# Second norm's factors stored with each row of attention's output; expert lists by one matmul a tile

## Chip, cores and metric

The kernel runs on one core of one Trainium2 chip. The time is that of one execution on the device, in microseconds (us). TensorE is PE, VectorE DVE, ScalarE ACT, GpSimd POOL, and SyncE, which here only issues DMAs, SP.

## The reference, cut to what matters

Rows of 256 floats (D) are embedded, go through attention with a residual, and then through a mixture of 8 experts, in which every expert takes the same number of rows (T / E):

```
h = tok(x)
h = h + attn(layernorm(h))                      # h1: 32 sequences x 512 tokens = 16384 rows
f = layernorm(h)                                # first norm of the expert layer: (x - m) / sqrt(v + eps)
norm = layer_norm(f, g, b)                      # second norm, of the rows already normed
scores = norm @ centroids.T
for e in range(8):                              # C = 2048 rows each, without those taken before
    s = where(taken, -inf, scores[:, e]); idx = top_k(s, C); taken[idx] = True
routed = f[idx]
out = routed + gelu(layer_norm(routed) @ w1 + b1) @ w2 + b2
h = h + out (put back at the rows' places)
```

Both norms are of the same row, so both come from one mean m and one variance v of the h1 row: y = (h1 - m) * ((1 + eps) v + eps^2)^-0.5 is what the expert's matmuls get (gain and bias g, b are put in later), and h1 * (1 + r) - m * r, with r = (v + eps)^-0.5, is what is added to the expert's result. These are the row's factors: two powers, and the two products with -m.

## The kernel before

All engines run in one program, each with its own instruction list, and hand over by semaphores (`wait_ge`). Work is in tiles of 128 rows (one row a partition); there are NT = 128 tiles, TS = 4 for each of the 32 sequences.

**Attention.** A loop over sequences; each step is a plan of ten halves (slots 0 to 9) written out by hand. The plan names tasks; PE makes them, ACT ("A") or DVE ("D") takes the result out of one of three PSUM banks. What the change touches is the task WO, the output product of a tile: tile 0 in slot 8, tiles 1, 2 and 3 in slots 0, 2 and 4 of the next step. In `dve_misc` (L1202 to L1218) DVE takes WO: it makes the tile's unscaled scores (L1206), h1 = residual + product (L1210), statistics (L1213), mean and variance (L1215), and stores (1 + eps) v + eps^2 in column n of `ve_all` (L1217). Before that DVE waits until the h1 buffer of two tiles ago is stored. SP (`store`) first issues, per half, the small transposed DMAs of MX tasks (`low`, L466 and L469), then the store of the h1 tile to `h1_rows` in HBM (L476), when DVE has made it. POOL's share of a step is, in this order, the gather of the next rows (L515, slots 5 to 8) and the norm of the step after next (`pool_norm`, L522, L528, L530, slots 6 to 9; its xn is what PE transposes at L784 in slot 0 of the next step).

**Between.** When all tiles are stored, POOL takes one power over all of `ve_all` (L621), DVE multiplies the scores by it (L1493), adds the constant (L1495), and then makes the list of the first expert alone (`dve_choice`): eight digits of 4 bits, for each a count of the rows over 15 candidates (L1251, 15 operations, summed over partitions by one PE matmul, L836), then cut, ties, positions, and the list. For the list DVE writes one-hot tensors of [128, 128 tiles, 16] bf16, ohP (place in the tile) and ohT (tile number) from ohA (L1292, L1295, L1296), and in 8 parts the tensor ohB of 16 tiles (L1302, two buffers). For each tile PE multiplies ohB's 128 columns as weights with ohP and with ohT (L857): 32 matmuls of 16 columns for each part, summed in one PSUM tile, which DVE converts to row numbers (`idx_next`, L1307).

**Experts.** Each of 8 experts has GR = 4 groups of GT = 4 tiles. For a group PE does 8 slots m of the first layer (L911; ACT's Gelu L728), then for each tile q the second layer (L924, slots 8 + q). While it does, the next group is prepared: POOL gathers its tiles (L539) into one half of `hrow`; DVE takes statistics of all four (`dve_stats`, L1322 to L1329) when they are there; POOL takes eight powers (`pool_power`, L583); DVE makes biases (`dve_scales`, L1333, L1334); ACT writes y and the residual part of each tile (`act_rows`, L700, L702); PE transposes y (`pe_rows`, L898), behind q = 0, 1 and 2, but for an expert's last group behind q = 2 and q = 3; ACT takes it out as hT (L717). DVE adds the residual to the result (`orow`, L1368), POOL adds b2 (L567) and scatters it (L571), and frees the buffer (L579), for which DVE waits.

The choice of the next expert's rows is spread over the slots by two tables, `pe_at` and `dve_at`. In groups 0 and 1: digits and counts, with the statistics in slot 5 and the scales in slot 7; slot 0 of each begins with a digit and a count right behind the last group's `orow`. In group 2: the rest of the choice, and the first list parts at slots 9 to 11. In group 3, slot 0, DVE does the last four parts and the numbers at once; PE has its parts in slots 0 to 3 and 5; statistics and scales come behind the first and second `orow`, and the gather of the next expert's first group waits for the numbers. So the order on each engine is fixed by hand.

## Time and profile before

| | us |
|---|---|
| median of 3 runs | 3180.93 (3177.55 to 3189.85) |
| the profiled execution | 3194.65 |
| its span | 3192.8 |
| PE busy | 2786.0 |
| DVE busy | 1804.9 |
| ACT busy | 1275.4 |
| POOL busy | 873.6 |

The span is what the profile's stretches and shares refer to; 1.85 us of the execution lie around it. PE is busy for 87% of the span, but matmuls are pipelined, so that does not say that it is at its peak. A row of a timeline gives start, length, engine and line, what is written and read, and in brackets the idle time of the engine before it with what ended it.

### The profile page before, as it was taken

The page shows a single profiled execution, that of the slowest core. Times are in us where ns is not written, and L with a number is a line of the kernel's source. Part 1 is how long each engine was busy: PE and PEld are TensorE (multiplying, and loading weights), DVE is VectorE, ACT ScalarE, POOL GpSimd, SP SyncE. Part 2 cuts the span into 40 slices and gives each one's busy share as a digit, 9 for nine tenths or more (in the row PEclk, how much of TensorE's full clock was granted, in tenths as well). Part 3 has the DMA queues.
Part 4 walks back from the last instruction along what each step waited for, and adds up shares of the span by engine and source line. Part 5 has one row for each costly group of instructions (what it writes and reads, how often), then busy time and mean ns, then how long its engine had stood idle before and what let it go on. Part 6 is the DMA issues. An engine that isn't in the chain of part 4 may idle for free. (4 is left out here: it accounts for less than half of the span.)

```text
span 3192.8 us, 118687 instructions
## 1 busy us (share of the span) xinstructions
PE 2786.0 (87%) x49160; PEld 1942.8 (61%) x49160; DVE 1804.9 (57%) x5978; ACT 1275.4 (40%) x2665; POOL 873.6 (27%) x938
## 2 busy tenths in 40 slices
PE   3899989989989989989989998059899999999998
PEld 1566666666666666666666666036565665655666
DVE  3555555555555555555556554667567676665720
ACT  1454444444444444444444442023333333343433
POOL 2212122122122112112112110224353443434443
PEclk9999999999999999999999998569999999999999
DMA  2000000000000000000000000000111101111020
GB/s 62 20 24 22 21 23 24 20 22 21 23 22 20 21 21 24 21 21 24 19 23 24 21 19 15 30 17 31 62 46 49 55 31 63 41 47 61 28 66 27
DMA packets 56398, 98.21 MB, mean 31 GB/s; under 512 B 10332, under 2 KB 41000, under 8 KB 55752
## 3 DMA queue, kind: packets, MB, share of 16 engines
q0 software_dynamic: 18624, 50.88, 5.6%
q1 hardware_dynamic: 37256, 40.07, 3.8%
q8 instruction: 368, 6.03, 0.8%
q14 instruction: 150, 1.23, 0.1%
HBM read 55.78 MB, written 33.55 MB: 28 GB/s over the span
## 5 line engine op out<-in xcount | busy, mean ns | idle before, releaser
L515 POOL DMA_INDIRECT rows<-in_tok_table,idx_now x132 | 138.0, 1045 | 1442.3 <-DVE hres L1154 1368.5
L911 PE MATMUL banks<-hT,w 128*128 128x512 f32 x1024 | 485.0, 622 | 16.1 <-ACT hT L717 12.1
L1176 DVE TENSOR_REDUCE mx<-banks 128x8 f32<-128x1024 f32 x256 | 301.5, 1219 | 204.3 <-PE banks L1014 200.9
L691 ACT ACTIVATE probT<-banks 128x1024 f32<-128x1024 f32 x256 | 262.6, 1026 | 229.8 <-PE banks L1058 229.8
L728 ACT ACTIVATE hid<-banks,b 128x512 f32<-128x512 f32 x256 | 175.2, 687 | 439.1 <-PE banks L911 439.0
L911 PEld LDWEIGHTS banks<-hT,w 128*128 128x128 f32 x1024 | 192.9, 197 | 229.6 <-issue 217.1
L1071 PEld LDWEIGHTS V_ps<-Ve,probT 128*64 128x64 f32 x4096 | 268.9, 147 | 24.9 <-issue 24.9
L1071 PE MATMUL V_ps<-Ve,probT 128*64 128x17 f32 x4096 | 281.8, 217 | 1.4 <-issue 1.4
L1071 PE MATMUL V_ps<-Vo,probT 128*64 128x17 f32 x4096 | 282.0, 217 | 0.2 <-issue 0.2
L1071 PEld LDWEIGHTS V_ps<-Vo,probT 128*64 128x64 f32 x4096 | 268.9, 147 | 0.3 <-issue 0.3
L1251 DVE TENSOR_SCALAR_CACHE_REDUCE hits<-act_s,cval 128x128 bf16<-128x128 f32 x960 | 261.6, 342 | 12.9 <-issue 10.7
L924 PE MATMUL M_ps<-w,hid 128*128 128x256 f32 x1024 | 233.3, 382 | 0.0
L924 PE MATMUL V_ps<-w,hid 128*128 128x256 f32 x1024 | 231.5, 380 | 0.0
L924 PEld LDWEIGHTS V_ps<-w,hid 128*128 128x128 f32 x1024 | 193.1, 190 | 38.4 <-issue 15.3
L924 PEld LDWEIGHTS M_ps<-w,hid 128*128 128x128 f32 x1024 | 191.8, 192 | 23.7
L1197 DVE TENSOR_TENSOR r<-M_ps,sg 128x256 f32<-128x256 f32 x128 | 54.4, 425 | 248.5 <-PE M_ps L799 247.6
L567 POOL TENSOR_TENSOR orow<-orow,b 128x256 f32<-128x256 f32 x128 | 127.1, 993 | 238.1 <-DVE orow L1368 236.7
L1052 PE MATMUL banks<-Qt,Kt 32*64 32x128 f32 x4096 | 184.7, 282 | 0.0
L657 ACT ACTIVATE low<-M_ps 8x256 f32<-8x256 f32 x128 | 47.7, 372 | 326.3 <-PE M_ps L793 326.3
L1052 PEld LDWEIGHTS banks<-Qt,Kt 32*64 32x64 f32 x4096 | 164.1, 132 | 22.7 <-issue 3.8
L571 POOL DMA_INDIRECT out_rows<-orow,idx_cur x128 | 144.4, 1128 | 110.5 <-POOL orow L567 77.3
L1054 PE MATMUL banks<-Qt,Kt 32*64 32x64 f32 x4096 | 173.4, 227 | 0.1
(228 smaller groups left out, 5885.3 us busy)
## 6 DMA issues: line engine op xcount, KB each, us to landing
h_rows<-h SPq DMA_DIRECT2D x128, 128.0 KB, 2.0
w<-in_w SPq DMA_DIRECT2D x16, 1024.0 KB, 5.9
Qt<-low SPq DMA_DIRECT2D x256, 4.0 KB
rows<-in_tok_table,idx_now POOLq DMA_INDIRECT x132, 3.5
out_rows<-orow,idx_cur POOLq DMA_INDIRECT x128, 2.5
cst<-in_tables SPq DMA_DIRECT2D x1, 1060.5 KB
Gq<-lowl SPq DMA_DIRECT2D x64, 8.0 KB
b<-in_b SPq DMA_DIRECT2D x8, 128.0 KB, 5.0
```

The source lines that it names most:

```text
L515: nc.gpsimd.indirect_dma_start(rows[:, t, :], None, ins["tok_table"], bass.IndirectOffsetOnAxis(idx_now[:, t:t + 1], 0)).then_inc(s_rows[t ...
L567: nc.gpsimd.tensor_tensor(out=orow[:, q % 2, :], in0=orow[:, q % 2, :], in1=b2[:, :], op=ALU.add).then_inc(s_add, 1)
L571: nc.gpsimd.indirect_dma_start(out, bass.IndirectOffsetOnAxis(idx_cur[:, g * GT + q:g * GT + q + 1], 0), orow[:, q % 2, :], None).then_inc ...
L691: nc.scalar.activation(dst[:, 2 * pair:2 * pair + 2, :], banks[:, 2 * pair:2 * pair + 2, :], ACT.Exp).then_inc(s_exp, 1)
L728: nc.scalar.activation(hid[:, m, :], S_ps[m % 2][:, 0:GT * P], ACT.Gelu_apprx_tanh, bias=b1[:, m:m + 1]).then_inc(s_hid, 1)
L911: mm = nc.tensor.matmul(S_ps[m % 2][:, 0:GT * P], w1[:, c, m * P:(m + 1) * P], hT[g % 2][:, c, :], start=c == 0, stop=c == KC - 1)
L924: mm = nc.tensor.matmul(O_ps[q % 2][:, 0:D], hid[:, m, q * P:(q + 1) * P], w2[:, m, :], start=m == 0, stop=m == FC - 1)
L1052: nc.tensor.matmul(banks[side[0], g, n * P:(n + 1) * P], k[:, W + at_:P + at_], q[:, at_:at_ + P], start=False, stop=n == G - 1)
L1054: nc.tensor.matmul(banks[side[1], g, n * P:n * P + W], k[:, at_:W + at_], q[:, at_:at_ + W], start=False, stop=False)
L1071: nc.tensor.matmul(V_ps[side[a], h * OW:(h + 1) * OW], probT[t % 2][:, g, n * P + a * W:n * P + (a + 1) * W], vals[:, t, h, :], start=True ...
L1176: nc.vector.tensor_reduce(tops.rearrange("p (g h) -> p g h", g=2), banks[:, 2 * pair:2 * pair + 2, :].rearrange("p g (h k) -> p g h k", h= ...
L1251: ins_ = nc.vector.tensor_scalar(hits[:, c, :], act_s[:, :], cval[:, c:c + 1].bitcast(F32), None, ALU.is_ge, ALU.add, accum_out=counts[:, ...
```

## The change

Each h1 row gets four more columns (1,040 bytes in place of 1,024): the two powers (the second with 1 added) and the two products with -m. DVE now writes both variances of the tile (`ve1`), and POOL, at the end of the slot of each WO, takes the two powers, the two products, the product of the tile's eight scores with the first power, and adds 1 (`pool_factors`). SP's store waits for this (`s_fac`). The factors come back with the gathered row, so `act_rows` waits for the gather itself and reads its scales and biases in the row; `dve_stats`, `dve_scales`, `pool_power` and the power over all tiles are gone, and the score product on DVE too: DVE waits for `s_score` of the last tile. ohP and ohT become the two halves of one tensor, ohN [128, 128 tiles, 2, 16], so that a list part is 16 matmuls of 32 columns, and the numbers are a copy of one half of PSUM and an addition of the other.

```diff
+RW = D + 4
...
-        h1_rows = nc.dram_tensor("h1_rows", [TOK, D], F32, kind="Internal").ap()
+        h1_rows = nc.dram_tensor("h1_rows", [TOK, RW], F32, kind="Internal").ap()
...
-        h1 = sb("h1", [P, 2, D])
+        h1 = sb("h1", [P, 2, RW])
...
-        mv1 = sb("mv1", [P, 2])
-        ve_all = sb("ve_all", [P, NT])
-        rs_all = sb("rs_all", [P, NT])
+        mv1 = sb("mv1", [P, 2, 2])
+        ve1 = sb("ve1", [P, 2, 2])
+        eps = sb("eps", [P, 2, 2])
...
-        ohP = sb("ohP", [P, NT, CT], BF16)
-        ohT = sb("ohT", [P, NT, CT], BF16)
+        ohN = sb("ohN", [P, NT, 2, CT], BF16)
...
-        hrow = sb("hrow", [P, 2, GT, D])
+        hrow = sb("hrow", [P, 2, GT, RW])
...
-        s_gr = [sem(f"s_gr{q}") for q in range(GT)]
-        s_var2 = sem("s_var2")
-        s_rs2 = sem("s_rs2")
-        s_scales = sem("s_scales")
+        s_gr = [[sem(f"s_gr{j}{q}") for q in range(GT)] for j in range(2)]
...
-                            sp.wait_ge(s_mD, m.out(task))
+                            sp.wait_ge(s_fac, TS * (b - lag(task)) + t + 1)
                             sp.dma_start(h1_tiles[:, bass.ds(TS * (b - lag(task)) + t, 1), :],
                                          h1[:, t % 2, :].unsqueeze(1)).then_inc(s_h1out[t % 2], 16)
...
+        def pool_factors(pool, n, t):
+
+            own = h1[:, t % 2, :]
+            pool.wait_ge(s_var1, n + t + 1)
+            nc.gpsimd.tensor_tensor(out=own[:, D:D + 2], in0=ve1[:, t % 2, :], in1=mhalf[:, :].to_broadcast([P, 2]),
+                                    op=ALU.pow).then_inc(s_rs1, 1)
+            pool.wait_ge(s_rs1, n + t + 1)
+            stand(pool)
+            nc.gpsimd.tensor_scalar(own[:, D + 2:D + 4], own[:, D:D + 2], mv1[:, t % 2, 0:1], -1.0,
+                                    ALU.mult, ALU.mult).then_inc(s_nm1, 1)
+            new = score[:, :, bass.ds(n + t, 1)]
+            nc.gpsimd.tensor_tensor(out=new, in0=new, in1=own[:, D:D + 1].unsqueeze(1).to_broadcast([P, E, 1]),
+                                    op=ALU.mult).then_inc(s_score, 1)
+            pool.wait_ge(s_nm1, n + t + 1)
+            stand(pool)
+            nc.gpsimd.tensor_scalar(own[:, D + 1:D + 2], own[:, D + 1:D + 2], 1.0, None, ALU.add).then_inc(s_fac, 1)
...
-                bass.IndirectOffsetOnAxis(idx[:, col:col + 1], 0)).then_inc(s_gr[q], 16)
+                bass.IndirectOffsetOnAxis(idx[:, col:col + 1], 0)).then_inc(s_gr[half][q], 16)
...
-                if g + 1 < GR:
-                    pool_power(pool, gi + 1)
...
-                    if (g, q) == (GR - 1, 1) and not last:
-                        pool_power(pool, gi + 1)
...
+                    for task in half:
+                        name, t = task
+                        if name == "WO" and m.here(task):
+                            pool_factors(pool, TS * (b - lag(task)), t)
...
-            pool.wait_ge(s_var1, NT)
-            nc.gpsimd.tensor_tensor(out=rs_all[:, :], in0=ve_all[:, :], in1=mhalf[:, :].to_broadcast([P, NT]),
-                                    op=ALU.pow).then_inc(s_rs1, 1)
...
-            pool_power(pool, 0)
...
-            if q == 0:
-                act.wait_ge(s_scales, gi + 1)
...
+            row = hrow[:, half, q, :]
+            act.wait_ge(s_gr[half][q], 16 * pair + 16)
             if q >= 2:
                 act.wait_ge(s_yT, GT * gi + q - 1)
-            nc.scalar.activation(y2[:, q % 2, :], hrow[:, half, q, :], ACT.Identity, scale=rs2[:, 0, q:q + 1],
-                                 bias=nmr[:, 0, q:q + 1]).then_inc(s_y2, 1)
-            nc.scalar.activation(hrow[:, half, q, :], hrow[:, half, q, :], ACT.Identity, scale=r1[:, q:q + 1],
-                                 bias=nmr[:, 1, q:q + 1]).then_inc(s_scaled, 1)
...
+            nc.scalar.activation(y2[:, q % 2, :], row[:, 0:D], ACT.Identity, scale=row[:, D:D + 1],
+                                 bias=row[:, D + 2:D + 3]).then_inc(s_y2, 1)
+            nc.scalar.activation(row[:, 0:D], row[:, 0:D], ACT.Identity, scale=row[:, D + 1:D + 2],
+                                 bias=row[:, D + 3:D + 4]).then_inc(s_scaled, 1)
...
-        LPS = M_ps[1][:, 0:CT]
+        LPS = M_ps[1][:, 0:2 * CT]
...
                 for j in range(LT):
-                    for half in (ohP, ohT):
-                        first_, last_ = k == 0 and j == 0 and half is ohP, k == LC - 1 and j == LT - 1 and half is ohT
-                        mm = nc.tensor.matmul(LPS, ohB[:, k % 2, j, :], half[:, k * LT + j, :],
-                                              start=first_, stop=last_)
+                    mm = nc.tensor.matmul(LPS, ohB[:, k % 2, j, :],
+                                          ohN[:, k * LT + j, :, :].rearrange("p a r -> p (a r)"),
+                                          start=k == 0 and j == 0, stop=k == LC - 1 and j == LT - 1)
                 mm.then_inc(s_used, 1)
...
-                  (2, 5): [("stats", 0)], (2, 6): [("list", 0)], (2, 7): [("scales", 0)], (2, Q0): [("places", 0)],
+                  (2, 6): [("list", 0)], (2, Q0): [("places", 0)],
                   (2, Q0 + 1): [("list", 1)], (2, Q0 + 2): [("list", 2)], (2, Q0 + 3): [("list", 3)],
-                  (3, 0): [("list", 4), ("list", 5), ("list", 6), ("list", 7), ("numbers", 0)],
-                  (3, Q0 + 1): [("stats", 0)], (3, Q0 + 2): [("scales", 0)]}
+                  (3, 0): [("list", 4), ("list", 5), ("list", 6), ("list", 7), ("numbers", 0)]}
...
-            dve_at[g, 5] = [("stats", 0)]
...
-            dve_at[g, 7] = [("scales", 0)]
...
-                chain(dve, nc.vector.bn_aggr(mv1[:, :], st1[:, :]), base)
-
-                nc.vector.tensor_scalar(ve_all[:, bass.ds(TS * bt + t, 1)], mv1[:, 1:2], 1.0 + EPS, EPS * EPS,
-                                        ALU.mult, ALU.add).then_inc(s_var1, 1)
+                chain(dve, nc.vector.bn_aggr(mv1[:, t % 2, :], st1[:, :]), base)
+
+                nc.vector.scalar_tensor_tensor(out=ve1[:, t % 2, :], in0=eps[:, 0, :], scalar=mv1[:, t % 2, 1:2],
+                                               in1=eps[:, 1, :], op0=ALU.mult, op1=ALU.add).then_inc(s_var1, 1)
...
-                nc.vector.tensor_scalar(ohP[:, :, :], ohA[:, :, :], c_part, None, ALU.mult)
-                nc.vector.scalar_tensor_tensor(out=ohT[:, :, :], in0=ohA[:, :, :], scalar=float(P),
+                nc.vector.tensor_scalar(ohN[:, :, 0, :], ohA[:, :, :], c_part, None, ALU.mult)
+                nc.vector.scalar_tensor_tensor(out=ohN[:, :, 1, :], in0=ohA[:, :, :], scalar=float(P),
                                                in1=laneb[:, 0:NT].unsqueeze(2).to_broadcast([P, NT, CT]),
                                                op0=ALU.mult, op1=ALU.mult).then_inc(s_ohA, 1)
...
-                nc.vector.tensor_copy(idx_next[:, :], LPS).then_inc(s_next, 1)
+                chain(dve, nc.vector.tensor_copy(rank[:, 0:CT], LPS[:, 0:CT]), base)
+                nc.vector.tensor_tensor(idx_next[:, :], rank[:, 0:CT], LPS[:, CT:2 * CT], ALU.add).then_inc(s_next, 1)
...
-        def dve_stats(dve, gi, half, base):
-            if not (isinstance(gi, int) and gi == 0):
-                dve.wait_ge(s_scaled, GT * gi)
-            for q in range(GT):
-                dve.wait_ge(s_gr[q], 16 * gi + 16)
-                nc.vector.bn_stats(st2[:, q, :], hrow[:, half, q, :])
-            chain(dve, nc.vector.memset(r1[:, :], 1.0), base)
-            stand(dve)
-            for q in range(GT):
-                ins_ = nc.vector.bn_aggr(mv2[:, q, :], st2[:, q, :])
-            chain(dve, ins_, base)
-            nc.vector.tensor_scalar(ve2[:, 0, :].unsqueeze(2), mv2[:, :, 1:2], 1.0 + EPS, EPS * EPS, ALU.mult, ALU.add)
-            nc.vector.tensor_scalar(ve2[:, 1, :].unsqueeze(2), mv2[:, :, 1:2], EPS, None, ALU.add).then_inc(s_var2, 1)
-
-        def dve_scales(dve, gi, base):
-            dve.wait_ge(s_rs2, gi + 1)
-            nc.vector.tensor_scalar(r1[:, :], rs2[:, 1, :], 1.0, None, ALU.add)
-            nc.vector.scalar_tensor_tensor(out=nmr[:, :, :], in0=mv2[:, :, 0].unsqueeze(1).to_broadcast([P, 2, GT]),
-                                           scalar=-1.0, in1=rs2[:, :, :], op0=ALU.mult, op1=ALU.mult)\
-                .then_inc(s_scales, 1)
...
+            for j in range(2):
+                nc.vector.memset(eps[:, 0, j:j + 1], (1.0 + EPS, 1.0)[j])
+                chain(dve, nc.vector.memset(eps[:, 1, j:j + 1], (EPS * EPS, EPS)[j]))
...
-            dve.wait_ge(s_rs1, 1)
-            chain(dve, nc.vector.tensor_tensor(score[:, :, :], score[:, :, :],
-                                               rs_all[:, :].unsqueeze(1).to_broadcast([P, E, NT]), ALU.mult), base)
+            dve.wait_ge(s_score, NT)
             chain(dve, nc.vector.tensor_tensor(score[:, :, :], score[:, :, :],
                                                kb[:, :].unsqueeze(2).to_broadcast([P, E, NT]), ALU.add), base)
...
-            dve_stats(dve, 0, 0, base)
-            dve_scales(dve, 0, base)
```

## Rows read from the trace of the kernel before

**Rows 1.** Stretches: busy us (instructions) of each engine, granted clock, DMA share, GB/s.

```profile
1000.00:1900.00 900.00, 825.48 (x20460) 596.34 (x20460) 500.48 (x1253) 405.51 (x886) 180.06 (x240) 0.95 0.08 22
2400.00:2800.00 400.00, 375.43 (x2045) 247.65 (x2044) 266.37 (x1198) 150.81 (x288) 175.90 (x155) 0.98 0.14 45
```

The engines of these columns are PE, its weight loads, DVE, ACT and POOL.

**Rows 2.** Timeline of DVE and POOL at attention's end (start us, length us).

```profile
2000.61 0.15 DVE L1217 TENSOR_SCALAR ve_all<-mv 128x1 f32<-128x1 f32 x1
2001.89 20.75 POOL L621 TENSOR_TENSOR rs_all<-ve_all,mhalf 128x128 f32<-128x128 f32 x1 [134.47 <-DMA h_rows<-h]
2022.78 1.22 DVE L1493 TENSOR_TENSOR score<-score,rs_all 128x1024 f32<-128x1024 f32 x1 [22.02 <-POOL rs_all L621]
```

**Rows 3.** Timeline before the first expert's first matmul.

```profile
2110.51 0.43 DVE L1322 BATCH_NORM_STATS2 st<-hrow 128x6 f32<-128x256 f32 x1 [0.83 <-DMA hrow<-h_rows,idx_next]
...
2118.16 0.60 ACT L700 ACTIVATE y<-hrow,nmr,rs 128x256 f32<-128x256 f32 x1
...
2120.86 1.22 PE L911 MATMUL banks<-hT,w 128*128 128x512 f32 x1 [1.36 <-ACT hT L717]
```

**Rows 4.** PE's waits in the expert stage, 2121 to 3192 (total us, times, longest).

```profile
PE M_ps L836 <- DVE hits L1251: 31.9, 17, 3.1
PE banks L898 <- ACT y L700: 12.2, 20, 2.2
```

**Rows 5.** Single lines over the whole run: count, duration ns min/median/max.

```profile
L522 POOL TENSOR_TENSOR rs<-ve,mhalf x128: 549/582/586, 53.9 to 1865.2; 128x1 f32<-128x1 f32 x128
L583 POOL TENSOR_TENSOR rs<-ve,mhalf x32: 1660/1672/3639, 2111.8 to 3139.5; 128x8 f32<-128x8 f32 x32
L1295 DVE TENSOR_SCALAR ohP<-ohA,cst x8: 753/753/754, 2081.1 to 3022.1; 128x2048 bf16<-128x2048 bf16 x8
L1302 DVE TENSOR_TENSOR ohB<-laneb,rlow x64: 2277/2283/2820, 2084.0 to 3044.3; 128x2048 bf16<-128x2048 bf16 x64
L1261 DVE TENSOR_TENSOR thr<-thr,delta x64: 158/160/1102, 2031.4 to 3004.0; 128x1 int32<-128x1 int32 x64
L1210 DVE TENSOR_TENSOR h<-hres,M_ps x128: 410/414/417, 135.0 to 1999.4; 128x256 f32<-128x256 f32 x128
```

**Rows 6.** Timeline of one attention step around the slots 8 and 9.

```profile
1020.26 0.15 DVE L1217 TENSOR_SCALAR ve_all<-mv 128x1 f32 x1
...
1022.41 0.19 POOL L528 TENSOR_TENSOR std<-ve,rs 128x1 f32<-128x1 f32 x1 [0.25 <-POOL rs L522]
1022.57 1.22 POOL L530 TENSOR_SCALAR xn<-hres,mv,rs 128x256 f32<-128x256 f32 x1
...
1032.89 0.48 PE L784 MATMUL M_ps<-cst,xn 128*128 128x128 f32 x1
```

**Rows 7.** Timeline of PE in the second expert: starts of short bf16 matmuls.

```profile
2329.78 0.23 PE L840 MATMUL M_ps<-equal,beforeb 128*128 128x128 bf16 x1
2329.84 0.22 PE L841 MATMUL M_ps<-equal,onesb 128*128 128x128 bf16 x1
...
2348.72 0.17 PE L857 MATMUL M_ps<-ohP,ohB 128*128 128x16 bf16 x1
...
2349.50 0.17 PE L857 MATMUL M_ps<-ohT,ohB 128*128 128x16 bf16 x1
```

**Rows 8.** Timeline of ACT and PE behind the Gelus of two groups.

```profile
2340.68 0.69 ACT L728 ACTIVATE hid<-banks,b 128x512 f32<-128x512 f32 x1 [1.03 <-PE banks L911]
2343.36 0.60 ACT L700 ACTIVATE y<-hrow,nmr,rs 128x256 f32<-128x256 f32 x1 [1.99 <-DVE nmr L1334]
2344.99 0.33 PE L898 MATMUL banks<-cst,y 128*128 128x128 f32 x1 [0.54 <-ACT y L700]
...
2387.15 0.60 ACT L700 ACTIVATE y<-hrow,nmr,rs 128x256 f32<-128x256 f32 x1 [9.30 <-DVE nmr L1334]
```

**Rows 9.** SP's waits in attention, 1000 to 1900 (total us, times, longest).

```profile
SPq L469 <- ACT low L657: 511.0, 60, 9.4
```

**Rows 10.** DMA issues: KB each, median us from issue to landing.

```profile
hrow<-h_rows,idx_next POOLq DMA_INDIRECT x64, 2.8
```

More of the change, by code:

```diff
@@ L190, in tower @@
         b1_all = sb("b1_all", [P, E, FC])
-        st2 = sb("st2", [P, GT, 6])
-        mv2 = sb("mv2", [P, GT, 2])
-        ve2 = sb("ve2", [P, 2, GT])
-        rs2 = sb("rs2", [P, 2, GT])
-        r1 = sb("r1", [P, GT])
-        nmr = sb("nmr", [P, 2, GT])
         wq = sba("wq", [P, KC, D])
@@ L319, in tower @@
         s_rs1 = sem("s_rs1")
+        s_nm1 = sem("s_nm1")
+        s_fac = sem("s_fac")
+        s_score = sem("s_score")
         s_std = sem("s_std")
@@ L692, in act_exp, with act_rows, act_group @@
                                  ACT.Exp).then_inc(s_exp, 1)
-        def act_rows(act, gi, q, half):
-            if q == 0:
-                act.wait_ge(s_scales, gi + 1)
+        def act_rows(act, gi, pair, q, half):
+            row = hrow[:, half, q, :]
+            act.wait_ge(s_gr[half][q], 16 * pair + 16)
             if q >= 2:
                 act.wait_ge(s_yT, GT * gi + q - 1)
-            nc.scalar.activation(y2[:, q % 2, :], hrow[:, half, q, :], ACT.Identity, scale=rs2[:, 0, q:q + 1],
-                                 bias=nmr[:, 0, q:q + 1]).then_inc(s_y2, 1)
-            nc.scalar.activation(hrow[:, half, q, :], hrow[:, half, q, :], ACT.Identity, scale=r1[:, q:q + 1],
-                                 bias=nmr[:, 1, q:q + 1]).then_inc(s_scaled, 1)
-        def act_group(act, gi, g):
-            act_rows(act, gi, 0, g % 2)
+            nc.scalar.activation(y2[:, q % 2, :], row[:, 0:D], ACT.Identity, scale=row[:, D:D + 1],
+                                 bias=row[:, D + 2:D + 3]).then_inc(s_y2, 1)
+            nc.scalar.activation(row[:, 0:D], row[:, 0:D], ACT.Identity, scale=row[:, D + 1:D + 2],
+                                 bias=row[:, D + 3:D + 4]).then_inc(s_scaled, 1)
+        def act_group(act, gi, pair, g):
+            act_rows(act, gi, pair, 0, g % 2)
             for q in range(GT):
                 if q + 1 < GT:
-                    act_rows(act, gi, q + 1, g % 2)
+                    act_rows(act, gi, pair, q + 1, g % 2)
                 act_transposed(act, gi, q, g)
@@ L730, in act_expert @@
                 if g + 1 < GR or not last:
-                    act_group(act, gi + 1, g + 1 if g + 1 < GR else 0)
+                    act_group(act, gi + 1, GR // 2 * e + (g + 1) // 2, g + 1 if g + 1 < GR else 0)
         @block.scalar
@@ L765, in _ @@
             nc.scalar.activation(scr[:, :], c_ident[:, 0:1], ACT.Copy).then_inc(s_hid, 2)
-            act_group(act, 0, 0)
+            act_group(act, 0, 0, 0)
             with act.Fori(0, E - 1) as e:
@@ L1343, in dve_expert @@
                 gi = GR * e + g
-                more = g + 1 < GR or not last
                 def parts(slot):
                     for part, k in dve_at.get((g, slot), []):
-                        if part == "stats":
-                            if more:
-                                dve_stats(dve, gi + 1, (g + 1) % 2, base)
-                        elif part == "scales":
-                            if more:
-                                dve_scales(dve, gi + 1, base)
-                        elif part == "numbers now":
+                        if part == "numbers now":
                             dve.wait_ge(s_free, 2 + CT * e)
@@ L1367, in dve_expert @@
                     dve.wait_ge(s_free, GT * gi + q + 1)
-                    nc.vector.tensor_tensor(orow[:, q % 2, :], O_ps[q % 2][:, 0:D], hrow[:, g % 2, q, :],
+                    nc.vector.tensor_tensor(orow[:, q % 2, :], O_ps[q % 2][:, 0:D], hrow[:, g % 2, q, 0:D],
                                             ALU.add).then_inc(s_fin, 1)
@@ L1500, in _ @@
                 dve_choice(dve, 0, part, k, base)
[L1501 to L1502 removed]
             base += CH["n"]
             CH["n"] = 0
[L1505 removed]
+            PER2 = 6 * DIGITS + 24
             with dve.Fori(0, E - 1) as e:
```

11 lines of the change are left out of this document (3 added, 8 removed).

## The prediction, made before the changed kernel ran

> **What bounds the kernel now.** I read the stages first, then the start of the expert stage as a chain, then what TensorE (PE) waits for in the experts. In attention (nearly 2,000 of the 3,192.8 us) PE is busy 825 of 900 us and POOL only 180; in the experts (from about 2,121 us) PE is busy 375 of 400 us. Between attention's last variance at 2000.61 and PE's first expert matmul at 2120.86 lie 120 us [rows 2, 3], in which PE has only the short matmuls of the choice. That stretch is one chain: POOL takes a power over all 128 tiles at once, 20.75 us, and DVE stood idle 22.02 us until it came; then DVE multiplies the scores, 1.22 us [rows 2], and chooses the first expert's rows with nothing beside it. Then four tiles are gathered; the last is there at 2110.51, but ACT writes its y only at 2118.16, because statistics, power and scales stand between; PE starts at 2120.86 [rows 3]. From there PE waits 31.9 us for the counts (DVE hits) and 12.2 us for y [rows 4]. So time is to be had where PE is short of work at the start, or where PE has less to do in the experts. DVE's work is worth nothing by itself.
>
> **The change, part by part.**
>
> 1. *The power over all tiles goes.* Last tile's variance is ready at 2000.61 + 0.15 = 2000.76 and the second score operation starts behind 2022.78 + 1.22 = 2024.00 [rows 2]. Now POOL does for this tile a power of 2 elements, a two-element product, then the 8-element score product, and DVE goes on at s_score. Power: 582 ns for 1 element and 1,672 for 8 [rows 5], 0.16 a further element, so 0.74. The wait behind it 0.25 and a small operation 0.19 [rows 6]. The score product has no row: between 0.19 (1 element) and 1.67 (8 elements of power); I take 0.3, since 256 elements take only 1.22 [rows 6]. Two hand-overs at 0.14 each (22.78 less 2001.89 + 20.75). Sum 1.8: DVE goes on at about 2002.5, gain **21.5** (20.1 to 21.6).
>
> 2. *Statistics of group 0 go.* ACT needs only the tile. y of the fourth tile starts at 2110.5 in place of 2118.16, and what follows it is the same; the other three are ready before. Gain **7.6** [rows 3]. The numbers cost one small DVE operation more (0.2), the last list part of PE is 0.4 shorter: **+0.2**. The first half of the one-hot tensor, 0.753 us now [rows 5], is written in runs of 16 elements; between 0.75 and the 2.28 of its neighbours of the same size without speed-up [rows 5]. I take 0.75, the runs being still contiguous; the end costs 1.5 once (in the other seven experts DVE is ahead there).
>
> 3. *Lists with one moving operand.* 8 experts x 8 parts x 32 matmuls become 16 of 32 columns. A part's 31 starts take 2349.50 - 2348.72 = 0.78 us, 25 ns each at 16 columns; with 128 columns two starts lie 60 ns apart [rows 7]. Straight between them 32 columns is 30 ns. If each column cost its share, 16 columns could not take 25 ns beside 60 for 128: a floor shows, so I take 25, part 0.80 to 0.40. The Trainium skill, "TensorE: Matmul & The Clock Gate", section "Wait — 56ns, not 53.3ns?", gives about 25 ns also for 32 columns; no row here shows it. The first expert's parts lie behind DVE's ohB (2.28 us each [rows 5]) and give nothing. The other 56 are in PE's own stream: 56 x 0.40 = **22.4** (17 at 30 ns, 0 if the price goes with columns). With list parts of 0.4 a slot on PE is 2.15 us (now 2.6), shorter than an ohB, so four parts in a row could catch up with DVE; but DVE has 3 us or more less ahead of them (statistics, the wait for scales), and enters group 3 earlier. I put nothing there; the end is 0.5 us in each of 7 experts, 3.5.
>
> 4. *Statistics, power and scales of the 31 other groups go.* DVE is lighter by some 3 us a group (four statistics of 0.43 [rows 3] and eight small operations), worth nothing as such: the long waits for hits come right behind a group's last orow (digit and count in slot 0), before the statistics, and stay. But ACT stands 1.99 us before y in one group and 9.30 us in the next for nmr [rows 8]; now it starts as its last Gelu ends (2341.37) or the gather lands. y of tile 1 is then ready three operations of 0.6 later, 2343.2, and PE asks for it at 2344.45 (2344.99 less its wait of 0.54 [rows 8]). So the y waits go: **12** of 12.2 [rows 4]. Next late are hT (the last two tiles' transposes directly before the next expert; unchanged) and hits. POOL also no longer holds a scatter behind var2.
>
> 5. *Attention, DVE.* One fused operation of 2 elements in place of one of 1, 154 ns [rows 6]: at most 0.08 x 128 off PE's path; DVE is busy 500 of 900 us [rows 1]. The setup gets four memsets, two waited for: **-0.4**, an estimate from small operations of 0.15 to 0.2; ends 0 and -1.
>
> 6. *Attention, POOL.* Four operations a tile, 0.74 + 0.25 + 0.19 + 0.3 + 0.25 + 0.19, about 1.9 us; 128 x 1.9 = 245 us on an engine that is 80% idle [rows 1]. Order matters: factors of tile 0 (slot 8) now stand before the norm of tile 3 (slot 9). Their variance is there at 1020.41; POOL is free of the second-last norm at 1021.6, so xn of tile 3 ends at 1023.8 + 1.9 = 1025.7, and PE reads it at 1032.89 [rows 6]: 7 us to spare. At the other slots POOL is idle. DVE itself waits for none of it before the end.
>
> 7. *SP and DMA.* The h1 store now waits for POOL, 2 us later. Behind it on SP is the next low store; SP waits 8.5 us on average for each of those (511.0 / 60 [rows 9]), which covers it. The buffer is wanted two tiles later, at 2,000 / 128 = 15.6 us a tile. Rows are 1,040 B in place of 1,024: gathers take 2.8 us to land [rows 10], issue paces them, and only group 0's last is exposed. The Trainium skill, "DMA: Bandwidth & Descriptors", section "How a descriptor splits into AXI transactions", speaks against such rows: rows that do not start at a 256-byte boundary fetch bytes they do not use, here up to a quarter more (an estimate from 1,040 B at such offsets). By that rule the last gather would land up to 0.7 us later and the sum be that much smaller; no row shows it.
>
> **Sum.** 21.5 + 7.6 + 0.2 + 22.4 + 12 - 0.4 = 63.3. The profiled execution took 3194.65 us and would take 3131.4. It lies 13.7 above the median of the runs, 3180.93; the gains are counts of work and not shares, so I take them off the median: **3118**.
>
> **Rivals.**
> - *Lists give nothing* (32 columns cost twice 16): for it, that no row has 32 columns; against it, the floor seen at 25 ns. 3194.65 - 40.9, or on the median 3140. Chance 0.08.
> - *DVE becomes what PE waits for in the experts*: the time cut from lists and y is waited for at the next count or ohB, so that only the start's 29.3 - 0.4 stays: 3152. For it, hits is already the largest wait [rows 4]; against it, its waits start at a group's end and no cut lies between that and the count. Chance 0.10.
> - *Slower: VectorE and POOL hold each other up in attention.* A DVE operation of 160 ns took 1,102 beside a POOL instruction, and a POOL power of 1.67 took 3.64 beside DVE [rows 5]. If each tile's factors held DVE up by 0.94 us where PE waits for h or the maxima, 128 x 0.94 = 120: 3118 + 120 = 3238. It decides from (63 + 16) / 128 = 0.62 us a tile, where the kernel would be slower by 0.5%. Against it: beside POOL's norms h took 410 to 417 ns, always [rows 5]. Chance 0.04. The Trainium skill's "GPSIMD Engine Reference", section "Specifications", says that the two share SBUF interfaces when DVE has two SBUF inputs or a 2-port mode, which is this mechanism; the trace agrees for the experts' 2,048-element operations and not for attention's.
> - *More than the sum*: with the lighter DVE and POOL a third of the hits waits goes too (10 of 31.9): 3108. Chance 0.10.
>
> **How the numbers follow.** The forecast has 0.68: its own range is 3110 to 3126 (lists at 30 ns, one-hot at 2.28, ohB 3.5: up; runs of before reach 3.4 below their median: down). The range 3103 to 3142 takes in the cases of more and of lists without gain. About 0.5%, 16 us, is what a measurement can tell from no change. All cases but the slower one gain over 16 us, less 0.03 for something unseen in attention that eats the gain: faster 0.93, same 0.03, slower 0.04.
>
> **What would show it.** Right: no POOL operation of 20 us before the scores, DVE's score operation 2 us behind the last variance; PE's first expert matmul 29 us nearer to attention's end; L857's successor 1,024 times, 25 ns apart; PE waits for y near nothing; hits near 30 us; attention's windows with the same PE busy and length. Wrong: matmul starts 50 ns apart, hits or ohB waits risen by 20 to 30 us, or a longer attention stage, with PE waiting for h or xn.

## The result, and the profile after

| | before | after |
|---|---|---|
| median of 4 runs each, us | 3185.39 (3177.55 to 3196.62) | 3092.39 (3087.99 to 3101.93) |
| profiled execution, us | 3194.65 | 3101.93 |
| expert stage (first first-layer matmul to the end), us | 1071.9 | 1007.4 |
| PE busy, us | 2786.0 | 2745.5 |
| DVE busy, us | 1804.9 | 1738.9 |
| POOL busy, us | 873.6 | 976.6 |

The ratio is 0.9709 (95%: 0.9668 to 0.9751): faster by 2.9%, 93 us. I had forecast 63 us and a range that ended at 3103; the measured 3092 lies 11 us below it. The direction was right and the size was not; about 30 us came from something that I had not counted. Those 30 lie in the expert stage: it gained 64.5 us where items 3 and 4 had 34.4. Attention's last variance starts at 2000.02, and before at 2000.61 [rows 2].

The two stretches of [rows 1], after the change:

```profile
1000.00:1900.00 900.00, 827.55 (x20700) 597.13 (x20699) 507.73 (x1264) 412.10 (x899) 270.02 (x484) 0.96 0.08 22
2400.00:2800.00 400.00, 385.33 (x1752) 252.29 (x1751) 257.52 (x1128) 161.87 (x306) 163.62 (x155) 0.99 0.16 51
```

In attention's 900 us POOL is busy for 90 us more; PE's busy time moves by 2 us and DVE's by 7, and attention does not end later. In the experts PE is busy 385 of 400 us (375 before).

Timeline of DVE and POOL at attention's end, which answers to [rows 2]:

```profile
2000.02 0.22 DVE L1215 SCALAR_TENSOR_TENSOR ve<-eps,mv 128x2 f32<-128x2 f32 x1
2000.33 0.72 POOL L531 TENSOR_TENSOR h<-ve,mhalf 128x2 f32<-128x2 f32 x1 [4.64 <-DVE ve L1215]
2001.26 0.27 POOL L535 TENSOR_SCALAR h<-h,mv 128x2 f32<-128x2 f32 x1 [0.20 <-POOL h L531]
2001.48 0.21 POOL L538 TENSOR_TENSOR score<-score,h 128x8 f32<-128x8 f32 x1
2001.83 1.22 DVE L1467 TENSOR_TENSOR score<-score,kb 128x1024 f32<-128x1024 f32 x1 [1.58 <-POOL score L538]
```

The power of 20.75 us is gone; DVE goes on 1.81 us behind the last variance's start, 1.59 behind its end, where I had 1.8.

Timeline before the first expert's first matmul, which answers to [rows 3]:

```profile
2085.97 0.60 ACT L702 ACTIVATE y<-hrow 128x256 f32<-128x256 f32 x1
...
2088.33 0.60 ACT L702 ACTIVATE y<-hrow 128x256 f32<-128x256 f32 x1 [0.58 <-DMA hrow<-h_rows,idx_next]
2088.84 0.58 ACT L704 ACTIVATE hrow<-hrow 128x256 f32<-128x256 f32 x1
...
2089.33 0.78 ACT L719 ACTIVATE hT<-banks,ln 128x128 f32<-128x128 f32 x2
2090.02 0.59 ACT L702 ACTIVATE y<-hrow 128x256 f32<-128x256 f32 x1
...
2092.71 1.21 PE L909 MATMUL banks<-hT,w 128*128 128x512 f32 x1 [1.36 <-ACT hT L719]
```

Here the fourth y does not start when its tile lands, as I had it: the third tile's y comes late, and its residual part and an hT stand on ACT between the two. From the numbers' first operation to PE's first matmul it takes 12.01 us in place of 18.09, a gain of 6.1 and not 7.6.

What PE waits for in the expert stage (2093 to the end), which answers to [rows 4]:

```profile
PE M_ps L838 <- DVE hits L1249: 20.5, 16, 1.9
PE banks L909 <- ACT hT L719: 12.1, 8, 1.6
PE banks L909 <- ACT hid L730: 1.1, 2, 0.8
```

y has left the table, as forecast. But hits (PE waiting for a count), which I said would stay at 31.9, stands at 20.5, and hid (PE waiting for a Gelu's result) fell from 4.0 to 1.1. That is the lead.

### The profile page after: what moved, and what is told of

Same layout as the page of the kernel before. It is cut to its first block and busy times, and to the rows that moved or that the text cites. A ratio compares the mean times of both kernels' runs of the same rounds, so it can differ in the third digit from the quotient of the medians.

```text
span 3100.1 us, 116908 instructions
## 1 busy us (share of the span) xinstructions
PE 2745.5 (89%) x48136; PEld 1915.2 (62%) x48136; DVE 1738.9 (56%) x5573; ACT 1277.5 (41%) x2665; POOL 976.6 (32%) x1417
## 5 line engine op out<-in xcount | busy, mean ns | idle before, releaser
L909 PE MATMUL banks<-hT,w 128*128 128x512 f32 x1024 | 477.6, 613 | 13.4 <-ACT hT L719 12.1
L531 POOL TENSOR_TENSOR h<-ve,mhalf 128x2 f32<-128x2 f32 x128 | 95.2, 744 | 916.8 <-DVE ve L1215 916.8
L922 PEld LDWEIGHTS M_ps<-w,hid 128*128 128x128 f32 x1024 | 190.3, 190 | 23.6
```

What stands on the lines that cost most here:

```text
L531: nc.gpsimd.tensor_tensor(out=own[:, D:D + 2], in0=ve1[:, t % 2, :], in1=mhalf[:, :].to_broadcast([P, 2]), op=ALU.pow).then_inc(s_rs1, 1)
L909: mm = nc.tensor.matmul(S_ps[m % 2][:, 0:GT * P], w1[:, c, m * P:(m + 1) * P], hT[g % 2][:, c, :], start=c == 0, stop=c == KC - 1)
L922: mm = nc.tensor.matmul(O_ps[q % 2][:, 0:D], hid[:, m, q * P:(q + 1) * P], w2[:, m, :], start=m == 0, stop=m == FC - 1)
```

## Where the missing 30 us are: one turn of the loop, side by side

PE's timeline at the third expert's start, the kernel before:

```profile
2394.67 3.70 PE L911 MATMUL banks<-hT,w 128*128 128x512 f32 x8 [1.56 <-ACT hT L717]
2398.87 1.99 PE L911 MATMUL banks<-hT,w 128*128 128x512 f32 x4 [0.51 <-ACT hid L728]
2403.93 0.20 PE L836 MATMUL M_ps<-counts,onesb 128*128 128x15 bf16 x1 [3.07 <-DVE hits L1251]
2404.01 8.31 PE L911 MATMUL banks<-hT,w 128*128 128x512 f32 x12
2412.16 0.17 PE L836 MATMUL M_ps<-counts,onesb 128*128 128x15 bf16 x1
```

and after the change:

```profile
2346.06 5.69 PE L909 MATMUL banks<-hT,w 128*128 128x512 f32 x12 [1.56 <-ACT hT L719]
2352.82 0.18 PE L838 MATMUL M_ps<-counts,onesb 128*128 128x15 bf16 x1 [1.07 <-DVE hits L1249]
2352.90 5.41 PE L909 MATMUL banks<-hT,w 128*128 128x512 f32 x12
2358.41 0.18 PE L838 MATMUL M_ps<-counts,onesb 128*128 128x15 bf16 x1
```

Two things differ. The wait for the first count is 3.07 and now 1.07. And the twelve matmuls behind it take 8.31 us before and 5.41 after: a loss that stands in no table of waits. The stretches of the kernel before show what it is (the last three columns are PE's granted clock, DMA share and GB/s):

```profile
2394.67:2404.00 9.33, 5.75 (x13) 2.19 (x13) 5.29 (x37) 3.23 (x4) 3.28 (x4) 0.95 0.44 145
2404.00:2406.00 2.00, 2.00 (x4) 0.97 (x5) 1.63 (x12) 0.00 (x0) 1.56 (x2) 0.50 0.45 131
2406.00:2408.00 2.00, 2.00 (x4) 0.89 (x3) 2.00 (x17) 0.17 (x1) 0.00 (x0) 0.50 0.23 66
```

Behind the long wait PE runs at a granted clock of 0.50 (1.2 GHz) for over 5 us. After the change the same place has 1.00. "Low clock" below is the sum of (1 - granted clock) over stretches of 1 us of the expert stage: 23.6 us before and 13.8 after. In the kernel before the clock fell at or just behind all six waits of about 3 us (in three of them before the wait had ended); after the change it fell behind none of those of 1.07; and it fell behind the waits of about 2 us in group 1 sometimes (three of seven before, five of seven after). That is no fixed rule: in a_shift25, below, it did not fall at one wait of 2.80 us. One fall costs PE about 1.4 us: group 1's first layer took 16.52 us before without one and 17.89 after with one, with the same wait in both.

Why is the count earlier? DVE's timeline at the same turn, before:

```profile
2396.55 0.17 DVE L1341 COPY b<-b_all 128x8 f32 x1 [3.42 <-issue]
...
2400.85 0.35 DVE L1251 TENSOR_SCALAR_CACHE_REDUCE hits<-act_s,cval 128x128 bf16<-128x128 f32 x1 [1.92 <-issue]
```

and after:

```profile
2347.45 0.17 DVE L1319 COPY b<-b_all 128x8 f32 x1 [2.92 <-issue]
```

At each turn DVE stands 3 to 4 us in front of the loop's first operation and waits for nothing that the profile shows. Before the change it stands a second time, 1.9 us, between the fourth and the fifth of 15 count operations, whose instructions did not change at all. In sum, for DVE over the expert stage of the kernel before:

```profile
DVE b L1341 <- issue: 21.5, 6, 4.1
...
DVE hits L1251 <- issue: 10.7, 6, 1.9
```

The second line is gone after the change; the first is 18.7. **Theory "place of the code":** DVE fetches its program in pieces; at a jump back the piece with the loop's start is fetched, and the next comes later. Before the change a piece ended some 22 instructions behind the loop's start, within the first count. The change took, by my count of the two programs, 25 instructions out ahead of the loop, so the piece reaches that much further, to a place where DVE waits for PE anyway. **Rival "lighter loop":** the gap went because statistics, scales and powers left the experts.

## Experiments

Labels with a_ start from the changed kernel, with b_ from the one before. Ratios are to the kernel before on the same chip. Attention's code is the same in all a_ kernels, yet its last mean and variance came anywhere from 1982.8 to 2012.2 us in their profiled executions; so medians carry several us of it, and I read sizes from the expert stage. That stage, the waits and the low clock are each read from one profiled execution, so a difference of a few us, of the size of two or three falls of the clock, is not to be leaned on.

| kernel | median us | ratio (95%) | expert stage, us | hits wait, us | low clock, us |
|---|---|---|---|---|---|
| before | 3185.4 | | 1071.9 | 31.9 | 23.6 |
| after | 3092.4 | 0.9709 (0.9668 to 0.9751) | 1007.4 | 20.5 | 13.8 |
| a_shift25 | 3123.9 | 0.9793 (0.9747 to 0.9839) | 1022.8 | 31.4 | 19.3 |
| a_shift64 | 3106.4 | 0.9736 (0.9704 to 0.9768) | 1007.8 | 21.1 | 13.8 |
| a_shift40 | 3127.3, one run | | 1032.4 | 42.4 | 19.6 |
| b_shift30 | 3169.6 | 0.9954 (0.9926 to 0.9982) | 1061.2 | 24.4 | 13.4 |
| b_lists | 3162.4 | 0.9918 (0.9887 to 0.9950) | 1055.0 | 30.8 | 16.9 |
| a_oldlists | 3122.5 | 0.9784 (0.9758 to 0.9810) | 1030.4 | 21.9 | 11.7 |
| a_slots | 3076.3 | 0.9648 (0.9623 to 0.9674) | 982.8 | 4.4 | 6.7 |
| a_turn | 3098.8 | 0.9721 (0.9687 to 0.9756) | 1007.1 | 14.1 | 22.3 |
| a_best | 3072.5 | 0.9614 (0.9584 to 0.9644) | 970.3 | 6.1 | 5.6 |
| b_slots | 3151.4 | 0.9902 (0.9885 to 0.9919) | 1042.5 | 10.7 | 5.8 |

### Moving the loop's code and nothing else

```diff
+        pad = sb("pad", [P, 25])
...
+            for j in range(25):
+                nc.vector.memset(pad[:, j:j + 1], 0.0)
             dve.wait_ge(s_score, NT)
```

**a_shift25.** 

> The changed kernel with 25 tiny memsets (128x1) of an unused tile on DVE, directly before DVE's wait for the last tile's scores, so that the code of the expert loop starts 25 instructions later in DVE's program, at the place (1,451st) that it has in the kernel before; nothing in the loop differs. The memsets themselves: 25 x 0.06 = 1.5 us, where DVE stands idle for 1.58. Theory 'place of the code': the gap of 1.8 us in the first count of each expert (DVE waiting for 'issue', 10.7 us in 6 times in the kernel before, none in the changed one) depends on where the loop's code lies. It comes back at the fifth of the 15 count operations, PE's wait for hits in group 0 goes from 1.07 to about 3, PE's granted clock falls to 0.50 behind it (1.7 us lost), so 6 x (1.8 + 0.3 + 1.7) = 23: 3115 us. Rival 'lighter loop': the gap went because statistics, scales and powers left the experts; then the memsets change nothing, 3092 to 3094, no issue gap in the count.

**a_shift64** (64 in place of 25). 

> The same with 64 memsets in place of 25. Direct cost 64 x 0.06 = 3.8 us less the 1.58 that DVE is idle: 2.3 us. Theory 'place of the code': if the gap comes where one piece of the code ends and the next has not arrived, the piece now ends before the loop's first instruction, no gap in the count, 3092 + 2.3 = 3095. Rival 'any longer program' (each added instruction ahead of the loop costs): gap at least as with 25 memsets, 3115 or more. Rival 'lighter loop': 3095 as well, so that only the pair with 25 memsets tells it from the first theory.

**b_shift30** (30, ahead of `dve.wait_ge(s_rs1, 1)` in the kernel before). 

> The kernel before with 30 memsets of an unused tile on DVE, directly before DVE's wait for the power over all tiles, where DVE stands idle for 22 us: they cost nothing. Theory 'place of the code': the piece of code that ends 22 instructions behind the loop's first one in the kernel before now ends before it; the gaps in the count (10.7 us in 6) go, hits waits fall by about 11 to about 21, the clock stays at 1.00 behind the first count of an expert, and the time is 3185 - 23 = 3162 (ratio 0.993). Rival 'lighter loop': 3185, gap and waits as before.

DVE's timeline at the third expert's start with 25 memsets:

```profile
2355.82 0.17 DVE L1320 COPY b<-b_all 128x8 f32 x1 [2.94 <-issue]
...
2359.94 0.09 DVE L1250 DVE_READ_ACCUMULATOR hits<-act_s,cval 128x1 bf16 x1 [1.49 <-issue]
```

With 25 tiny memsets, executed once, 90 us ahead of the experts, the gap is back, now in front of the read behind the fifth count operation; the loop's code is the same. Hits waits rise to 31.4 and the expert stage by 15.4 us. With 64 the gap is absent and the stage is 1007.8 against 1007.4. In the kernel before, 30 take the gap away and bring 10.7 us. "Lighter loop" foresaw no effect in the first and third and is out. The medians go the same way: b_shift30's ratio, 0.9954, has 1 outside its interval. That of a_shift64, 3106.4, is 11 us over the 3095 that I expected; its attention was 12 us longer than the changed kernel's in the profiled executions.

My sizes were too large (23 foreseen, 15.4 and 10.7 measured). I took 1.7 us for a fall of the clock, which costs 1.4. With 25 memsets the low clock also rose by only 5.5 us, where six falls of 1.7 would be 10.2: at two of the six first counts the clock stayed up, and it fell behind four of group 1's waits where it had fallen behind five. In b_shift30 the waits in group 0 fell by 11.2 us, as foreseen (17.6 to 6.4), and the low clock by 10.2; but the waits in group 1 rose from 1.9 to about 2.35 us each, 3 us in sum, and those for y, hid, ohB and equal by 3.5 together.

**a_shift40** (40 memsets). 

> The changed kernel with 40 memsets. With 25 the issue gap stood after the fifth count operation, 23 instructions behind the loop's first one when each count operation is counted as two (the operation and the read of its sum). Theory 'place of the code': with 15 more it stands 8 instructions behind the first one, before cand (L1246), again six times and 1.6 us long; the count is as late as with 25, so the expert stage is 1022 to 1026 us (1022.8 with 25, 1007.8 with 64). Rival 'the gap belongs to the count operations' (their own pipeline, the load of the DMA queues at that time): it stays between count operations, or does not appear.

DVE's timeline there, third expert:

```profile
2350.32 0.17 DVE L1320 COPY b<-b_all 128x8 f32 x1 [2.94 <-issue]
...
2354.33 0.17 DVE L1246 TENSOR_TENSOR cand<-digits,thr 128x15 int32<-128x15 int32 x1 [3.45 <-issue]
```

The place is right to the instruction, but the gap is not 1.6 us: it is 3.4 to 3.7, and the stage 10 us longer than with 25 memsets. The rows tell why. From b's copy to the end of the gap it is 4.01 us here, 4.12 with 25 memsets and 4.30 in the kernel before (4.0 to 4.3 at nearly all turns). So the next piece comes about 4 us behind the loop's start, wherever the piece ends; the nearer its end, the longer DVE stands. The DMA view of the kernel before for 2397 to 2401 has this line, a transfer of instructions (8 KB) within the gap:

```profile
q14 instruction: 1, 0.01, 0.5%
```

The traces' single packets show more. At each of the six turns, in all twelve kernels, a packet of this queue starts 1.6 to 2.5 us behind the first operation. In all 30 turns with a gap (before, a_shift25, a_shift40, b_lists, b_slots) DVE goes on 1.85 to 1.93 us after that packet's start, and a second packet starts within 5.0 us; in the kernels without a gap there is no second one so soon. The DMA view for the 5 us behind b's copy, in the kernel before (2396.5 to 2401.5) and after (2347.4 to 2352.4):

```profile
q14 instruction: 2, 0.02, 1.0%
q14 instruction: 1, 0.01, 0.5%
```

That DVE waits for this transfer is thus more than a guess from the gap's place, though the queue's lines do not name the engine that it serves.

The Trainium skill, "Runtime: NRT & Kernel Launch", section "Instruction fetch mechanics", says that instructions come by DMA in blocks, and that a taken branch to a target outside the window forces a fetch. The wait at each turn and the gap's place agree with it. It also says that crossing a block's end is mostly hidden; behind a jump it was not here, 0.9 to 3.7 us each time.

### The two halves of the change

```diff
-                    for half in (ohP, ohT):
...
-                        mm = nc.tensor.matmul(LPS, ohB[:, k % 2, j, :], half[:, k * LT + j, :],
-                                              start=first_, stop=last_)
+                    mm = nc.tensor.matmul(LPS, ohB[:, k % 2, j, :],
+                                          ohN[:, k * LT + j, :, :].rearrange("p a r -> p (a r)"),
+                                          start=k == 0 and j == 0, stop=k == LC - 1 and j == LT - 1)
```

**b_lists** (the lists alone, in the kernel before). 

> The kernel before with the lists alone changed (one tensor ohN, 16 matmuls of 32 columns a part, the numbers by a copy and an addition). Theory 'parts of 0.40': in PE's own stream 7 x 8 parts take 0.40 in place of 0.81 us, 56 x 0.41 = 23: 3185 - 23 = 3162; hits waits 31.9, issue gaps in the count 10.7 and y waits about 12 stay. Rival 'lists did more': the shorter lists alone also shortened the hits waits or the y waits, 3185 - 23 - 10 or more = 3152 or less. Rival 'DVE holds the list': PE catches up with DVE's ohB in group 3 and waits there, 3185 - 15 = 3170 or more.

**a_oldlists** (the changed kernel with the lists as they were). 

> The changed kernel with the lists as before (ohP and ohT, 32 matmuls of 16 columns a part, the numbers by one copy). With the lists alone changed in the kernel before, the expert stage (first expert matmul to the end) fell by only 16.9 us, 6.7 of it clock, since PE then waited 13.0 us for DVE's ohB in place of 1.2. Theory 'the statistics hold DVE': without them DVE is ahead with ohB, so the lists are worth their whole 56 x 0.41 = 23 us here: 3115 us, expert stage 1007.4 + 23 = 1030, ohB waits near nothing. Rival 'DVE holds PE here too': the lists are worth 10 to 15 us, 3105, with ohB waits in the changed kernel; against it, its trace has none.

What PE waits for in b_lists' expert stage, and below it the list parts on PE in the changed kernel:

```profile
PE M_ps L835 <- DVE hits L1249: 30.8, 15, 2.8
PE M_ps L854 <- DVE ohB L1300: 13.0, 14, 1.8
PE banks L909 <- ACT hT L716: 12.1, 8, 1.6
PE banks L896 <- ACT y L699: 11.5, 20, 1.8
```

```profile
2439.42 0.56 PE L857 MATMUL M_ps<-ohN,ohB 128*128 128x32 bf16 x16
2439.82 1.96 PE L909 MATMUL banks<-hT,w 128*128 128x512 f32 x4
2441.62 0.55 PE L857 MATMUL M_ps<-ohN,ohB 128*128 128x32 bf16 x16
```

Sixteen matmuls of 32 columns start within 0.40 us, 25 ns each, exactly the price at 16 columns. (The Trainium skill, "TensorE: Matmul & The Clock Gate", section "Wait — 56ns, not 53.3ns?", gives that figure for 32 columns; the trace agrees.) Put back in the changed kernel the long lists cost 23.0 us, what was expected. But alone, in the kernel before, the short ones bring 16.9 us of the expert stage, although the low clock also fell by 6.7: PE catches up with DVE and waits 13.0 us for ohB where it had waited 1.2. So the rival "DVE holds the list" had the mechanism for that kernel; its time, 3170 or more, did not come (the median is 3162.4, the theory's value, with attention's scatter in it). The lists bring 16.9 us of the stage alone and the rest of the change 41.5 (a_oldlists), together 64.5: worth some 6 us more together than apart. That this is because statistics and scales no longer hold DVE fits the ohB waits, none in the changed kernel, but is not shown by a run of its own.

### What was left: where PE asks, and the turn

**a_slots.** 

> The changed kernel with PE's first two counts of groups 0 and 1 one slot later (slots 3 and 6 in place of 2 and 5); DVE's program is the same to the instruction. If the waits for hits (20.5 us: 1.07 in group 0 and 1.92 in group 1 of each expert) and the clock at 0.50 behind the longer of them (8.5 us lost between the first expert's start and the end of the run) are what remains, then a slot of 1.76 us covers the first, and the second goes with it: hits waits about 5, 3092 - 15.5 - 8.5 = 3068, granted clock 1.00 from the first expert's second group to the end. Rival 'DVE is the bound': the wait comes back at the next count (slot 6, 9 or 11), 3085 to 3092.

```diff
-            for n, slot in enumerate((2, 5, Q0 + 1, Q0 + 3)):
+            for n, slot in enumerate((3, 6, Q0 + 1, Q0 + 3)):
```

**b_slots** (the same line in the kernel before). 

> The kernel before with PE's first two counts of groups 0 and 1 one slot later (3 and 6), as in a_slots. If the hits waits and the clock drops behind them are a matter of where PE asks, most of what I had left standing in the forecast was to be had without the change: hits 31.9 less 1.76 x 6 and 1.76 x 7, about 10 left; of the clock's loss in the expert stage (23.6) about 5 stay for start and end and 1.7 for a y wait: 1071.9 - 22 - 17 = 1033 us for the stage, 3185 - 39 = 3146. Rival 'DVE is the bound in the kernel before': with statistics and scales in DVE's stream the later counts push ohB and y, waits there rise by 10 us or more, stage 1043 or more, 3156 or more.

PE's waits in the expert stage, a_slots:

```profile
PE banks L909 <- ACT hT L719: 12.1, 8, 1.6
PE M_ps L838 <- DVE hits L1249: 4.4, 19, 0.4
PE banks L909 <- ACT hid L730: 1.4, 2, 1.1
```

One slot later, two numbers in a table, is worth 24.6 us of the stage (24 foreseen): 16.1 of waits, and the clock stays at 1.00 from 6 us into the stage to its last 8 us. The median, 3076.3, is 16 us under the changed kernel's where I had 24, with attention's scatter in both. In the kernel before it brings 29.4. I expected 39; the hits waits (10.7) and the clock (5.8) came out as foreseen. Priced at 1.4 a fall the sum is 36, and waits elsewhere (y, hid, equal) rose by 3.1 us; the last 3 us I cannot assign.

**a_turn.** 

> The changed kernel with the transposes of the next expert's first group behind q = 0, 1 and 2, as in all other groups (they stood behind q = 2 and 3): y of tile 1 is written 0.8 us before q = 0 ends. PE's wait of 1.56 us for hT at each turn and 0.2 of the transposes' own tail go: 7 x 1.78 = 12.5. Theory 'the turn on DVE sets the count': DVE's wait of 2.8 to 3.7 us for its own code at the turn stays where it is, so PE is 1.78 earlier at slot 2 and waits that much longer for hits (1.07 to 2.85, 10.7 us in 6), for hid about 0.5 (3 us), and the granted clock falls behind it (6 x 1.7 = 10): 3092 - 12.5 + 10.7 + 3 + 10 = 3103. Rival 'the wait for hT is simply saved': 3080.

```diff
-                        for r in ([], [], [0, 1], [2, 3])[q]:
+                        for r in ([0, 1], [2], [3], [])[q]:
```

PE's waits in its expert stage:

```profile
PE banks L909 <- ACT hid L730: 14.4, 6, 2.9
PE M_ps L838 <- DVE hits L1249: 14.1, 11, 1.9
PE banks L909 <- ACT hT L719: 1.4, 1, 1.4
```

The waits for hT are gone, 10.7 us, and the stage is as long as before, 1007.1: everything came back. It came back as waits for hid, not hits as I had it, and as low clock, from 13.8 to 22.3. By the program, b's copy, which ACT's Gelu needs, stands behind the same turn on DVE and is asked for earlier than the count.

**a_best.** 

> Both edits, with room for the turn: the transposes behind q = 0, 1 and 2, PE's first two counts at slots 4 and 7 in group 0 and 3 and 6 in group 1, and the copy of b1 for the next expert taken out of the turn (behind the first orow of group 3). Expected: hits waits about 5, no wait for hT but the first, none for hid: 3092 - 24 - 12.5 = 3056. Rival 'the count's delay reaches the lists': DVE is late with ohB in groups 2 and 3, waits there of 10 us or more, 3066 or more.

```diff
-            for n, slot in enumerate((2, 5, Q0 + 1, Q0 + 3)):
+            for n, slot in enumerate((4 - g, 7 - g, Q0 + 1, Q0 + 3)):
...
-                        for r in ([], [], [0, 1], [2, 3])[q]:
+                        for r in ([0, 1], [2], [3], [])[q]:
...
+                    if (g, q) == (GR - 1, 1) and not last:
+                        dve_bias(dve, e + 1)
```

(`dve_bias` is the wait for s_hid and the copy of b1, moved out of the loop's start.) PE's waits in its expert stage:

```profile
PE M_ps L838 <- DVE hits L1249: 6.1, 15, 0.9
PE banks L909 <- ACT hT L719: 1.4, 1, 1.4
```

The expert stage is 970.3, 37.1 less than in the changed kernel (36.5 foreseen); the rival's waits for ohB did not come. The median, 3072.5, is 3.9% under the kernel before and beats both kernels, but I had expected 3056. Between the two ratios lie 1.0%, some 30 of the 37 us; attention, 12 us longer in its profiled execution than in the changed kernel's, blurs the rest.

## Why the prediction was wrong, point by point

Of the 92.7 us between the two profiled executions:

| step | forecast, us | measured, or estimated from rows, us |
|---|---|---|
| 1: power over all tiles | 21.5 | 21.6 |
| 2: statistics of group 0, numbers | 7.8 | 5.9 |
| 3: lists | 22.4 | 23.0 |
| 4: y waits | 12 | 17.8 |
| 4: hits "stay" | 0 | 11.4 |
| hid, ohB, equal | 0 | 4.4 |
| PE's clock | 0 | 7.9 |
| 5 and 6: attention | -0.4 | 0.6 |

The table's five lines for the expert stage add up to its 64.5 us more closely than they are known: the lists' 23.0 holds for the changed kernel, the clock's 7.9 is an estimate, and the same way of adding gives 18.5 for b_lists, where 16.9 was measured.

- **The failed step is item 4's "the long waits for hits come right behind a group's last orow ..., before the statistics, and stay".** I took a wait whose producer's work does not change for one that cannot change. I had not read DVE's own idle time within the count, where 10.7 us stood as "issue". The hits waits fell by 11.4 us. Moving the code back to its old place (a_shift25) brings them back to 31.4 and gives back 15.4 us of my error of 29. My rival "more than the sum" had the size (10 of 31.9) but the wrong cause, the lighter DVE and POOL.
- **The clock had no term.** 9.8 us less at low clock, at about 0.8 of it in PE's time (1.4 of 1.7 for one fall), gives 7.9. In a_shift25 5.5 of low clock, over 4 us by this price, came back with the gap; the rest I did not take apart.
- **y waits** were mis-sized. Each costs more than its row says. PE's timeline of the kernel before, second layer to second layer:

```profile
2479.85 0.44 PE L898 MATMUL banks<-cst,y 128*128 128x128 f32 x2
2480.83 0.44 PE L898 MATMUL banks<-cst,y 128*128 128x128 f32 x2 [0.54 <-ACT y L700]
2481.11 1.25 PE L924 MATMUL M_ps<-w,hid 128*128 128x256 f32 x5
```

  From the first transpose to the next layer it is 1.26 us, and 0.43 after the change: 0.83 for a wait of 0.54. Added over the trace's 86 places where PE transposes y in the expert stage, the time from the start of the matmul ahead of the transposes to the start of the one behind them is 70.9 us before and 53.1 after: 17.8, of which 12.2 stood as waits.
- **Item 2** lost 1.5: the fourth y stands behind ACT's own chain and does not start at its tile's landing. In four of the eight traces with the change the third y waited 0.55 to 0.58 for its tile, in one 0.23 and in three not at all; from the numbers to PE's first matmul it took 11.4 to 12.1 us in these eight.
- **Items 1 and 3 held.** A power of 2 elements took 0.72 (0.74 foreseen), the score product 0.21 (0.3). **Items 5 and 6** came to nothing that can be measured: attention's 0.6 lies far within the 30 us by which its end scatters, and that the two profiled executions (92.7 apart) agree so well with the medians (93.0) is partly luck. h stayed at 410 to 416 ns in attention, so the rival of VectorE and POOL holding each other up did not come about there. But h reads one of its inputs from PSUM, so its rows, which I had counted against that rival, say nothing of operations with two inputs in SBUF.
- **Item 7:** the rows' store took 0.7 us longer to land (2.0 before), which nothing waited for; the gathers' median stayed at 2.8:

```profile
h_rows<-h SPq DMA_DIRECT2D x128, 130.0 KB, 2.7
```

  By the rule of the Trainium skill that I weighed ("DMA: Bandwidth & Descriptors", section "How a descriptor splits into AXI transactions") rows that start off a 256-byte boundary fetch bytes that they do not use. The median of the gathers shows no cost; whether the store's 0.7 us has this cause, no run here shows.

What stays open: why the turn itself became shorter (DVE's wait in front of b's copy 21.5 to 18.7); why hid, ohB and equal fell by 4.4, which no run took apart; and at which waits of 1.9 us or more the clock falls.

## What to carry to other kernels

Look at the bounding engine's waits, then at what their producer did in the same microseconds: a producer that stands for "issue" just behind a loop's jump, with a packet of an instruction queue in the same microseconds, may be waiting for its code, as here, and any edit ahead of the loop can move or remove that gap. Before crediting a change, shift the code by a few dozen harmless instructions, in both kernels. And where one engine asks for another's result right behind a loop's turn, ask a slot later: that was worth 25 us here for two numbers in a table, half as much again as its waits, in good part because PE's clock no longer fell.

## What the runs showed of the hardware that I had not expected

- DVE waited 2.6 to 4.4 us in front of the first operation at each jump back of a loop of some 350 to 400 operations a turn (as traced), and a second wait, where there was one, ended 3.5 to 4.3 us behind that operation and 1.85 to 1.93 us after the start of an 8 KB instruction transfer. Eight instructions behind the loop's start it was 3.4 to 3.7 us long, at 21 to 23 instructions 0.9 to 1.9, and in the changed kernel with 64 memsets or none it was absent.
- 16 matmuls of 128 x 32 bf16 columns, each with its own weights, started 25 ns apart, as those of 16 columns did.
- A granted clock of 0.50 at or behind PE waits of 1.9 to 3.1 us, for some 3 to 7 us, cost 1.4 to 2.9 us that no table of waits shows. It did not follow each of these waits.
